# Second-norm squares ahead of the transfers, expert weight split moved, attention units regrouped

## What is computed

```
h = W[x] + positions
h = h + linear_attention(layernorm(h))            # 8 heads, elu + 1 features
h = h + block(layernorm(h))                       # the block changed here
h = h + spectral_mixer(layernorm(h))              # FFT convolution with filters af
h = h + (layernorm(h) @ weight.T + bias)

block(x):  f = rmsnorm(x); q, k, v = f @ wq.T, f @ wk.T, f @ wv.T   # 4 query heads, 2 key heads of 16
           q, k = rope(q), rope(k)
           y = softmax(causal(q k^T) / 4) @ v;  x = x + y @ wo.T
           softmax router over 8 experts, top 2, gated experts with w1, w3, w2
```

## Time and profile before

| what | us |
|---|---|
| median of 3 runs | 391.57 |
| lowest, highest run | 388.62, 395.94 |
| the profiled execution, its own time | 391.39 |
| its span in the trace | 389.6 |
| TensorE busy in the span | 320.7 (82%) |
| VectorE busy | 251.6 (65%) |
| ScalarE busy | 144.4 (37%) |
| GpSimd busy | 107.4 (28%) |
| mean granted TensorE clock | 0.912 of full |

### The profile page before, as it was taken

One profiled execution on the slowest core, in us unless ns is written; L12 is line 12 of the kernel. 1 busy time (PEld: TensorE's weight loads), 2 busy tenths in 40 slices (PEclk: granted clock), 3 DMA queues, 4 the chain that ended last, 5 costly groups with the idle time before them and its releaser, 6 DMA issues.

```text
span 389.6 us, 4320 instructions
## 1 busy us (share of the span) xinstructions
PE 320.7 (82%) x1552; PEld 177.4 (46%) x1563; DVE 251.6 (65%) x414; ACT 144.4 (37%) x238; POOL 107.4 (28%) x138
## 2 busy tenths in 40 slices
PE   1348787779999989779999999998699961599994
PEld 0125563423334332365855355555355530267744
DVE  1498657888977730217596456653879999853385
ACT  2123435521665748023255444453364000012160
POOL 5790000262422214000001212221202988700000
PEclk9998999955999999758699999999899998599998
DMA  7949200274000000000000000000000000000001
GB/s 268 302 142 423 101 1 0 34 134 78 1 3 1 3 3 0 2 0 0 2 1 0 2 0 2 1 0 3 0 0 0 2 0 0 0 0 1 2 0 54
DMA packets 6166, 15.22 MB, mean 39 GB/s; under 512 B 1282, under 2 KB 3714, under 8 KB 5506
## 3 DMA queue, kind: packets, MB, share of 16 engines
q1 hardware_dynamic: 5410, 14.24, 11.5%
q0 software_dynamic: 512, 0.53, 0.6%
q10 hardware_dynamic: 224, 0.20, 0.3%
HBM read 12.02 MB, written 0.52 MB: 32 GB/s over the span
## 4 chain that ended last, share of the span: by engine, by line
PE 59%; DVE 17%; POOL 9%; ACT 7%; issue 6%; DMA 1%; ACTq 0%; SPq 0%; DVEq 0%; POOLq 0%
PE ps L296 57%; POOL arena L468 2%; POOL arena L469 2%; DVE arena L1515 1%; POOL e_lo L400 1%; DVE arena L1516 1%; POOL share L468 1%; DVE arena L1424 1%; POOL share L469 1%; DVE rw L1357 1%; PE ps L479 1%; DVE st L1184 1%; DMA idt<-ident 1%; ACT L941 1%; DVE arena L1500 1%
## 5 line engine op out<-in xcount | busy, mean ns | idle before, releaser
L296 PE MATMUL ps<-arena 96*128 96x512 bf16 (+6 forms) x192 | 49.3, 369 | 4.6 <-DMA arena<-arena 3.6
L1054 ACT ACTIVATE arena<-ps 128x1024 f32<-128x1024 f32 (+3 forms) x48 | 37.9, 812 | 36.9 <-PE ps L296 36.3
L1357 DVE TENSOR_REDUCE rw<-ps 128x1 f32<-128x512 f32 (+3 forms) x78 | 45.6, 641 | 7.9 <-PE ps L296 7.9
L296 PE MATMUL ps<-bfc_s 128*128 128x512 bf16 (+2 forms) x168 | 44.7, 380 | 1.7 <-DVE tmp L1322 1.3
L296 PE MATMUL ps<-xs,e_hi 128*128 128x512 f32 x96 | 41.0, 427 | 0.2 <-ACT arena L1080 0.2
L1424 DVE TENSOR_TENSOR arena<-ps,arena 128x512 f32<-128x512 f32 x48 | 33.0, 691 | 11.2 <-ACT arena L1080 10.8
L296 PE MATMUL ps<-xs,e_lo 128*128 128x512 f32 x96 | 38.8, 404 | 0.0
L1080 ACT ACTIVATE arena<-ps 128x512 f32<-128x512 f32 x48 | 28.7, 598 | 26.1 <-PE ps L296 21.9
L296 PE MATMUL ps<-arena,tk_s 128*128 128x384 f32 x64 | 24.7, 542 | 13.9 <-DVE arena L1500 12.6
L296 PEld LDWEIGHTS ps<-arena 96*128 96x128 bf16 (+1 forms) x192 | 16.8, 105 | 36.7 <-DVE rw L1357 17.7
L296 PE MATMUL ps<-w,xT 128*128 128x128 f32 (+3 forms) x128 | 27.1, 370 | 2.5 <-DVE xT L1387 1.6
(11 more groups left out here) (228 smaller groups left out, 521.1 us busy)
## 6 DMA issues: line engine op xcount, KB each, us to landing
w<-wpack SPq DMA_DIRECT2D x1, 2152.5 KB
arena<-arena SPq DMA_DIRECT2D x22, 96.0 KB, 2.8
arena<-tm SPq DMA_DIRECT2D x2, 1024.0 KB, 5.9
arena<-epack SPq DMA_DIRECT2D x1, 1540.0 KB, 11.1
arena<-rope SPq DMA_DIRECT2D x1, 1024.0 KB
tu_s<-tu SPq DMA_DIRECT2D x2, 512.0 KB, 12.0
tk_s<-tk SPq DMA_DIRECT2D x2, 512.0 KB, 13.6
rp<-rpack SPq DMA_DIRECT2D x1, 678.5 KB, 4.2
```

Source lines behind the costliest of these rows:

```text
L296: return nc.tensor.matmul(o, l, r, start=start, stop=stop, **kw)
L1054: nc.scalar.activation(pt[:, n % PT_SLOTS, :, lo:512], ps[:, bank:bank + 2, lo:512], ACT.Exp, scale=HD ** -0.5).then_inc(S("exp_done"), 1)
L1357: V.tensor_reduce(top_view(m, part)[:, at:at + len(heads), i], src, AXX, ALU.max, negate=True).then_inc(S("ring_read"), 1)
```

## The change

The squares of the second norm go ahead of all transfers. `EARLY_AF` falls from 7 to 5. VectorE's `e_hi` copy goes from behind the last q piece into the second norm, between the centred rows and the sums of squares. ScalarE's load of the exp function goes from ahead of the T2 evacuation to behind the last transfer. `piece(5)` comes ahead of two transfer copies and `piece(6)` right behind them. The first top unit (four heads) becomes two of two heads, so there are seven top units; `TOP_OF` follows. The stacks are issued in another order and gathered by seven semaphores, one for each top unit. The filler ahead of the row items grows from 4 to 12 matmuls. The lines that make `ORDER` stay as they are.

```
--- before.py
+++ after.py
@@ -43,7 +43,7 @@
                                              "wpc_zero", "k_ones"))}
 NORMS = {"var1": 1, "var2": 2, "msq2": 3, "var2b": 4, "var3": 5, "var3b": 6, "var4": 7,
          "std1": 1, "std2": 2, "rms2": 3, "rms2b": 4, "std3": 5, "rms3b": 6, "std4": 7}
-EARLY_AF = 7
+EARLY_AF = 5
...
@@ -66,7 +66,7 @@
     DUOS[2 * _d + 2, 1] = _d
 DUOS[ALL_PAIRS - 1, 2] = ALL_PAIRS // 2 - 1
 
-TOP_UNITS = [(0, 0, (0, 1, 2, 3)), (0, 1, (0, 1)), (0, 1, (2, 3)), (1, 1, (0, 1)), (1, 1, (2, 3)), (1, 0, (0, 1, 2, 3))]
+TOP_UNITS = [(0, 0, (0, 1)), (0, 0, (2, 3)), (0, 1, (0, 1)), (0, 1, (2, 3)), (1, 1, (0, 1)), (1, 1, (2, 3)), (1, 0, (0, 1, 2, 3))]
...
@@ -84,10 +84,11 @@
 
 
 COL_UNITS = [(0, 0, 0), (0, 0, 1), (0, 1, 0), (0, 1, 1), (1, 1, 0), (1, 1, 1), (1, 0, 0), (1, 0, 1)]
-TOP_OF = [0, 0, 1, 2, 3, 4, 5, 5]
+TOP_OF = [0, 1, 2, 3, 4, 5, 6, 6]
 COL_STEPS = [(k, j) for k, (_, c, _) in enumerate(COL_UNITS) for j in range(4 * c + 4)]
 UNIT_END = [sum(4 * c + 4 for _, c, _ in COL_UNITS[:k + 1]) for k in range(len(COL_UNITS))]
 PT_SLOTS = 8
+WARM = 12
...
@@ -125,6 +126,7 @@
             UNIT_END[5] + 6: [("y", 1, 1)], UNIT_END[5] + 7: [("yT", 1, 0), ("o", 1, 0)]}.get(step, [])
 
 
+STACKED = (48, 48, 48, 48, 64, 64, 64)
 PV_LAG = 6
 ORDER = list(RING[:COLS_FROM])
 _todo = list(RING[COLS_FROM:])
@@ -320,33 +322,36 @@
             for s in range(2):
                 sp.dma_start(tk_s[:, s], tk[s]).then_inc(ld_k, 16)
 
-            def stack_q(b, c, done):
-
-                for hh in range(NH):
+            def stack_q(b, c, heads, done):
+
+                for hh in heads:
                     at = 16 * (b * NH + hh)
                     sp.dma_start(qst[0:MROW, c, b * NH + hh],
                                  pieces_q[c][at:at + 16].rearrange("p n t -> p (n t)")).then_inc(done, 16)
 
-            def stack_k(b, c, done):
-
-                for g in range(NKV):
-                    at = 64 * c + 16 * (b * NKV + g)
-                    sp.dma_start(kst[0:MROW, b * NKV + g, c * 512:(c + 1) * 512],
-                                 pieces_k[at:at + 16].rearrange("p n t -> p (n t)")).then_inc(done, 16)
+            def stack_k(b, c, g, done):
+
+                at = 64 * c + 16 * (b * NKV + g)
+                sp.dma_start(kst[0:MROW, b * NKV + g, c * 512:(c + 1) * 512],
+                             pieces_k[at:at + 16].rearrange("p n t -> p (n t)")).then_inc(done, 16)
 
             sp.wait_ge(S("q_pieces"), 1)
             sp.wait_ge(S("copies"), 1)
-            stack_q(0, 0, S("stacks0"))
+            stack_q(0, 0, (0, 1), S("stacks0"))
+            stack_q(0, 0, (2, 3), S("stacks1"))
             sp.wait_ge(S("k_pieces"), 1)
             sp.wait_ge(S("copies"), 2)
-            stack_k(0, 1, S("stacks1"))
+            for g in range(NKV):
+                stack_k(0, 1, g, S("stacks%d" % (2 + g)))
             sp.wait_ge(S("q_pieces"), 2)
             sp.wait_ge(S("copies"), 3)
-            stack_q(0, 1, S("stacks1"))
-            stack_k(1, 0, S("stacks2"))
-            stack_k(1, 1, S("stacks2"))
-            stack_q(1, 1, S("stacks2"))
-            stack_q(1, 0, S("stacks3"))
+            for g in range(NKV):
+                stack_q(0, 1, (2 * g, 2 * g + 1), S("stacks%d" % (2 + g)))
+            stack_q(1, 0, range(NH), S("stacks6"))
+            for c in range(2):
+                for g in range(NKV):
+                    stack_k(1, c, g, S("stacks4"))
+            stack_q(1, 1, range(NH), S("stacks5"))
             for m, (b, c, heads) in enumerate(TOP_UNITS):
                 sp.wait_ge(S("ring_read"), RING_ORDER.index(("top", m, 0)) + 1)
                 lo, n = b * NH + heads[0], len(heads)
@@ -411,7 +416,7 @@
                 if c == 0:
                     pool.wait_ge(S("ring_read"), RING_ORDER.index(("rows", m, len(ROW_ITEMS[m]) - 1)) + 1)
                 else:
-                    pool.wait_ge(S("top_all"), m)
+                    pool.wait_ge(S("top_all"), m - 1)
                 if m >= 2:
                     pool.wait_ge(S("ring"), RING_ORDER.index(("top", m - 2, 0)) + 1)
                 step(nc.gpsimd.tensor_copy(pcs[:, 0], x))
@@ -600,7 +605,7 @@
             pe.wait_ge(S("rope_read"), 6)
             pe.wait_ge(ld_bf, 16)
             pe.wait_ge(S("constants"), CONSTANTS["k_ones"])
-            keep_warm(4, 1)
+            keep_warm(WARM, 1)
 
             taken = [0]
 
@@ -616,9 +621,10 @@
 
                 b, c, _ = TOP_UNITS[m]
                 i, heads, key0, wd, part = ROW_ITEMS[m][n]
-                if n == 0 and m in (0, 1, 3, 5):
-                    group = (0, 1, 3, 5).index(m)
-                    pe.wait_ge(S("stacks%d" % group), (96, 96, 128, 64)[group])
+                if n == 0:
+                    pe.wait_ge(S("stacks%d" % m), STACKED[m])
+                    if m == 4:
+                        pe.wait_ge(S("stacks5"), STACKED[5])
                 bank = ring_bank()
                 for x, hh in enumerate(heads):
                     ins = mm(ps[:, bank, x * wd:(x + 1) * wd], qst[0:MROW, c, b * NH + hh, i * P:(i + 1) * P],
@@ -986,17 +992,15 @@
                 nc.scalar.copy(dst.rearrange("p d c -> p (d c)").rearrange("p (x c) -> p x c", x=2),
                                ps[:, bank:bank + 2, 0:288]).then_inc(S("af_done"), 1)
 
+            squares(1, xc)
             for n in range(EARLY_AF):
                 af_copy(n, (2, 6, 4)[n % 3])
-
-                if n == 2:
-                    squares(1, xc)
+                if n == 0:
                     act.wait_ge(S("mean_squares"), NORMS["var2"])
                     nc.scalar.activation(st[:, 3], st[:, 2], ACT.Sqrt).then_inc(S("roots"), 1)
-                if n == 4:
+                if n == 1:
                     act.wait_ge(S("mean_squares"), NORMS["msq2"])
                     nc.scalar.activation(st[:, 6], st[:, 5], ACT.Sqrt).then_inc(S("roots"), 1)
-            next_function(ACT.Exp)
             evac(2, S("T2"), 1, S("xT2_lo"), scale=W("ln1"))
 
             def piece(n, value, pcs, slots, part, src):
@@ -1014,22 +1018,19 @@
             act.wait_ge(S("k_pieces"), 1)
             act.wait_ge(S("copies"), 2)
             for g in range(NKV):
-                act.dma_start(kst[0:MROW, g, 0:512], pieces_k[16 * g:16 * g + 16].rearrange("p n t -> p (n t)")).then_inc(S("stacks0"), 16)
+                act.dma_start(kst[0:MROW, g, 0:512],
+                              pieces_k[16 * g:16 * g + 16].rearrange("p n t -> p (n t)")).then_inc(S("stacks%d" % g), 16)
+            piece(5, 3, pieces_q1, Q_SLOTS, 0, qr[:, 512:N])
             for n in range(EARLY_AF, EARLY_AF + 2):
                 af_copy(n, (2, 4)[(n - EARLY_AF) % 2])
+            piece(6, 3, pieces_q1, Q_SLOTS, 1, tmp[:, 512:N])
             act.wait_ge(S("v2"), 1)
             act.wait_ge(S("constants"), CONSTANTS["va2_ones"])
             nc.scalar.copy(va2[:, :, :, :, 0:HD],
                            ps[:, 7].rearrange("p (j b k d) -> p j b k d", j=NT, b=B, k=NKV)).then_inc(S("va2"), 1)
-            late = list(range(EARLY_AF + 2, 2 * NK + 1))
-            for n in late[:3]:
+            for n in range(EARLY_AF + 2, 2 * NK + 1):
                 af_copy(n, (2, 4)[(n - EARLY_AF) % 2])
-            piece(5, 3, pieces_q1, Q_SLOTS, 0, qr[:, 512:N])
-            for n in late[3:4]:
-                af_copy(n, (2, 4)[(n - EARLY_AF) % 2])
-            piece(6, 3, pieces_q1, Q_SLOTS, 1, tmp[:, 512:N])
-            for n in late[4:]:
-                af_copy(n, (2, 4)[(n - EARLY_AF) % 2])
+            next_function(ACT.Exp)
             act.wait_ge(S("af_done"), 1)
             nc.scalar.copy(afx[:, 0], af[:, 0, 0]).then_inc(S("af_done"), 1)
 
@@ -1043,9 +1044,8 @@
 
             for n, (k, j) in enumerate(COL_STEPS):
                 act.wait_ge(S("cols"), n + 1)
-                if n == 0:
-                    for group, value in enumerate((96, 96, 128, 64)):
-                        act.wait_ge(S("stacks%d" % group), value)
+                for group in {0: (0, 1, 6), 1: (2, 3, 4), 3: (5,)}.get(n, ()):
+                    act.wait_ge(S("stacks%d" % group), STACKED[group])
                 if n == 4:
                     act.wait_ge(S("e_split"), 3)
                 if n >= PT_SLOTS:
@@ -1183,7 +1183,7 @@
                     dve.wait_ge(S("squared"), 2 * i + n + 1)
                     step(V.tensor_reduce(hst(1, a), half3(sq, a), AXX, ALU.add))
 
-            def centre(i, var_sem, complete=None):
+            def centre(i, var_sem, complete=None, between=None):
 
                 for a in range(2):
                     if complete:
@@ -1191,6 +1191,8 @@
                     step(V.tensor_reduce(hst(0, a), half3(h, a), AXX, ALU.add))
                     V.scalar_tensor_tensor(out=half3(xc, a), in0=spread(hst(0, a), 2, C), scalar=-1.0 / C, in1=half3(h, a),
                                            op0=ALU.mult, op1=ALU.add).then_inc(S("centred"), 1)
+                if between:
+                    between()
                 square_sums(i)
```

(12 more changed lines are left out.)

50 lines of the change are left out of this document (26 added, 24 removed).

## The result

The changed kernel takes 414.74 us (median of 4 runs, 407.61 to 418.13), the kernel before 392.06 beside it (388.62 to 395.94). Its ratio to the kernel before is 1.048, 95% interval 1.030 to 1.067: slower, some 7 us beyond the forecast of 408.0 and inside its range. Two of the four runs (417.47 and 418.13) are in a slower state, and ratios here are taken without such runs; the other two have a mean of 409.8. The profiled execution took 412.01, its span is 410.3 us against 389.6, so 20.7 us are to be found.

The account below looks back on a forecast made before the run. TensorE was taken as the bound, busy 52.9 of 56.6 us from 104 to 160.6. From 391.4: -4.0 front, +1.7 moved items, +13.2 stalls, +5.7 clock = 408.0 us, range 396 to 418.

Parts of the forecast that it names:

- Norm and pieces: From the second norm to the first column step: earlier squares and q pieces gain 4.0 us (2.0 to 5.1).
- Moved items: Seven ring items move into the stage where TensorE is full, costing 1.7 us.
- The waits: TensorE waits for the maxima's DMA ahead of five units' first column steps: 13.2 us in all (11 to 20).
- The clock: TensorE's idle in the five stalls lowers its clock in the column stage, costing 5.7 us.
- The chance of a fall: Two of three TensorE idle times of this size lose the full clock, applied to five stalls.
- The stalls cost little: Rival, chance 0.12: VectorE and ScalarE catch up while TensorE waits, so it ends faster, 389.1 or 386.6 us.
- The clock holds: Rival, chance 0.17: the stalls come but TensorE's clock stays full, 399.8 us.
- The clock stays low for long: Rival, chance 0.09: TensorE's clock stays low for 17.0 us, twice, 419 us.

Follow-up runs that it names:

- split_late: The changed kernel with the e_hi copy back behind the last q piece: 411.16 us, a single run.
- early_filled: The changed kernel with columns starting 13 instead of 8 items behind the first top, plus unread filler matmuls where TensorE idles: 382.4 us, ratio 0.980.
- early11_filled: The changed kernel with columns starting 11 instead of 8 items behind the first top, plus unread filler matmuls where TensorE idles: 387.01 us, ratio 0.990.
- fill_stalls: The changed kernel with 12 unread matmuls ahead of the wait for the maxima at the first step of units 2 to 6: 404.24 us, ratio 1.037.
- warm4: The changed kernel with 4 filler matmuls ahead of the row items instead of 12: 411.91 us, ratio 1.052.
- seven_in_before: The kernel before with only the first top unit split in two, making seven units: 422.64 us, ratio 1.087.

## Why the prediction was right, step by step

- **Norm and pieces.** Forecast: transposes near 61.3, last q piece near 77.3, first column step near 90, gain 4.0. Measured 61.06, 77.09 (L1341 starts at 76.40, 0.69 long), 89.87, gain 4.4. The rows of before placed these to 0.4 us. The e_hi copy at the norm cost 0.9 (split_late), where I had 1.2. One detail was other: the grant was 0.5 from 75.6 to 79.0, behind the idle of 3.02 ahead of 74.93, so the filler ran partly at half, and the first top (85.96) waited for VectorE's reductions: e_lo ended at 84.10 and the first step of top_pieces began 0.80 later.
- **Moved items**, 1.7: not measured alone; early_filled against early11_filled can't tell it from the waits.
- **The waits**, the step that decided. Forecast 2.8 for each of four and 2.1 for the fifth, 13.2 in all. The order of the list, the place of the five waits and what they wait for came as forecast. Measured 3.0 to 3.1 for the four and 2.7 for the fifth, five together 15.1, and the wait for GpSimd ahead of the last top grew from 1.00 to 1.78, which I had left as it was. The size was off mainly by the landing: I took 1.65 us behind the issue, the chain shows 1.92, which makes 1.35 of the 1.9 over five waits. The Trainium skill, DMA: Bandwidth & Descriptors, "Anatomy of one DMA", has about 2.0 for the fixed part, for the software path, while this DMA is issued by SyncE. The 1.92 of the trace is nearer to that than to my value, and the sum by the page, an estimate, would have been 15.0.
- **The clock.** Forecast 5.7, as three or four falls of 3.4 us low in a full TensorE. Measured: it fell with all five waits, low for 33.1 us; the fifth fall has GpSimd's wait of 1.78 just ahead of it as well. The spans leave 20.7 + 4.4 - 1.7 - 15.1 - 0.8 = 7.5 for it, worked out, not measured. It is less than half of the 30.5 us that TensorE was busy in those stretches, 15.3, partly because the attention's end, low in the kernel before for 17.0 us, ran at full clock this time. fill_stalls puts it at 6 to 10. My term was too low for two reasons that the trace shows: all five waits lost the clock where I had counted two of three, and I took the shortest low stretch for all, while two lasted 6.4 to 6.6 and one 13.4. That 7.5 still lies near the 5.7 is partly luck: the full clock at the attention's end was not forecast, and it made up for a part.
- **The chance of a fall.** My two of three rested on three idle times. Over the four profiled executions that have these waits without filler in them, the clock fell with 17 of 20, between 1.9 us before the wait's end and 1.7 behind it: all five in the changed kernel and in split_late, four in warm4, three in seven_in_before. Waits of 3.1 us stand on both sides, so their length alone doesn't decide it.
- **Rivals.** "The stalls cost little" is refuted by fill_stalls: VectorE and ScalarE could clear what they owed there and 12.8 us were still lost. "The clock holds" was built as a kernel: 404.2, where the rival said 399.8. "The clock stays low for long" came in part. The range of 396 to 418 held 414.7. The errors of the terms on the profiled 412.0 nearly all lie on one side: 1.9 and 0.8 too little for the waits, 1.8 for the clock, and the front gained 0.4 more. Together that is 4.1, and 4.0 are missing.

## What to carry to other kernels

Where an order of work is generated from a list, a change of the list's units moves every item that others wait for, even if the generator isn't touched: write down how far each producer stands ahead of its consumer, before and after, in time and not in steps. A producer whose result goes over two engines and a DMA needs its whole way covered (3.3 us here), and the last narrow steps cover less than the wide ones. When an in-order TensorE has to wait anyway, a few matmuls into a bank that is free kept its clock in four of five waits here, worth 6 to 10 us beside 15.1 us of waiting.

## What had not been expected of the hardware

The landing of a 6 KB DMA within the core's memory took 1.92 us, of a 96 KB one 2.8 (median), both from the start of the issue. The clock, once lost, came back at very different times although TensorE was busy nearly all the time: after 3.3, 3.4, 6.4 and 13.4 us in one execution (busy 3.30, 3.40, 6.38 and 12.38 of them). From 85.9 to 96.0 it stayed low although TensorE was busy 9.92 of 10.1 us. And equal waits did not have equal consequences: with a wait of 3.1 us the clock fell in the changed kernel (3.11, ahead of 103.02) and not in seven_in_before (3.10, ahead of 125.79); an idle time of 1.94 lost it and one of 2.41 did not in the kernel before.
